# Another order of the steps on all engines: values of two head groups and the router product next to each other

## The reference

```python
def _L0_xattn_ref(query, key, value, Wq, bq, Wk, bk, Wv, bv, We, be, Wo, bo):
    Q = (query @ Wq.T + bq)...; K = (key @ Wk.T + bk)...; V = (value @ Wv.T + bv)...
    scores = jnp.einsum('bhqd,bhkd->bhqk', Q, K) / jnp.sqrt(jnp.asarray(DK, Q.dtype))
    attn = jax.nn.softmax(scores, axis=-1)
    out = jnp.einsum('bhqk,bhkd->bhqd', attn, V)
    expert = (jnp.einsum('bsd,eod->ebso', out, We) + be[:, None, None, :]).mean(axis=0)
    return expert @ Wo.T + bo

def _L0_ffn_ref(x, w_gate, w_expert, b_expert):
    probs = jax.nn.softmax(hs @ w_gate, axis=1)
    best = jnp.argmax(probs, axis=1)
    locations = jnp.cumsum(mask, axis=0) - 1      # only the first 100 rows of an expert count
    ...
    expert_out = dispatched @ w_expert + b_expert
    combined = combine.reshape(-1, E * C) @ expert_out

x = x + jnp.tanh(g_xattn[0]) * _L0_xattn_ref(_layernorm(x), ctx_1024, ctx_1024, ...)
x = x + jnp.tanh(g_ffn[0]) * _L0_ffn_ref(_layernorm(x), ...)
```

## Time and profile before

| | |
|---|---|
| median of 3 runs | 405.21 us (405.14 to 405.38) |
| the profiled execution: its own time | 405.64 us |
| its span, first to last instruction | 403.9 us, 8706 instructions |
| PE busy | 396.3 us (98%) |
| DVE busy | 333.3 us (83%) |
| ACT busy | 225.3 us (56%) |
| POOL busy | 167.4 us (41%) |
| granted TensorE clock | full in all 40 slices |

### The profile page before, as it was taken

The page is one execution under the profiler, slowest core; times in us unless marked ns, Lnnn a source line. Parts: engine busy times, 40 slices in busy tenths (PEclk is TensorE's granted clock), DMA queues, the critical chain, the costliest instruction groups (busy, mean ns, idle before and its releaser), DMA issues.

```text
span 403.9 us, 8706 instructions
## 1 busy us (share of the span) xinstructions
PE 396.3 (98%) x3102; PEld 182.2 (45%) x3102; DVE 333.3 (83%) x662; ACT 225.3 (56%) x320; POOL 167.4 (41%) x157
## 2 busy tenths in 40 slices
PE   7999999999999999999999999999999999899996
PEld 4556454443444444444444434444444444354444
DVE  6548456986898989998998998899897589779996
ACT  4436323568566754947485486748556474775110
POOL 2028999215080247309033530713271064460371
PEclk9999999999999999999999999999999999999999
DMA  8999991466059408823960692295169016241585
GB/s 278 334 389 394 344 390 41 91 124 165 2 111 199 174 1 170 217 98 85 175 223 1 142 238 104 60 183 189 54 133 242 5 33 175 84 132 28 99 172 180
DMA packets 65901, 63.19 MB, mean 156 GB/s; under 512 B 42277, under 2 KB 45617, under 8 KB 65859
## 3 DMA queue, kind: packets, MB, share of 16 engines
q1 hardware_dynamic: 60747, 56.19, 50.9%
q0 software_dynamic: 1632, 3.49, 3.1%
q10 hardware_dynamic: 3480, 2.96, 2.2%
HBM read 29.59 MB, written 12.98 MB: 105 GB/s over the span
## 4 chain that ended last, share of the span: by engine, by line
PE 71%; DVE 2%; issue 1%; ACT 1%; POOL 1%; DVEq 0%; ACTq 0%; POOLq 0%
PE ps L840 71%; ACT probs L1234 1%; PE ps L1161 0%; DVE xb L1567 0%; POOL known L1929 0%; POOL rstd L1929 0%; DVE bn_raw L1573 0%; ACT xn_hi L1234 0%; DVE xn L1500 0%; DVE base_cnt L1653 0%; DVE place_hot L1723 0%; POOL veps L1927 0%; ACT part_x L1234 0%; DVE xb L1865 0%; DVE wqT_lo L1678 0%
## 5 line engine op out<-in xcount | busy, mean ns | idle before, releaser
L1234 ACT ACTIVATE probs<-ps 120x1024 f32<-120x1024 f32 x64 | 62.0, 1024 | 19.4 <-PE ps L840 19.4
L1602 DVE TENSOR_REDUCE neg_max<-ps 128x16 bf16<-128x1920 f32 x32 | 68.7, 2148 | 3.7 <-PE ps L840 3.7
L1989 POOL TENSOR_TENSOR attn_lo<-attn,attn_hi 128x512 f16<-128x512 f32 x28 | 31.8, 1158 | 91.0 <-ACT attn_hi L1234 91.0
L840 PE MATMUL ps<-xnT_hi,wqT_hi 128*128 128x512 f16 x128 | 48.6, 380 | 0.0
L840 PE MATMUL ps<-mixT_hi,attn_hi 128*128 128x512 f16 x128 | 48.5, 379 | 0.0
L840 PE MATMUL ps<-mixT_lo,attn_hi 128*128 128x512 f16 x128 | 48.5, 379 | 0.0
L840 PE MATMUL ps<-xnT_lo,wqT_hi 128*128 128x512 f16 x128 | 48.5, 379 | 0.0
L1997 POOL TENSOR_TENSOR xb<-xb,mix_bias 128x512 f32<-128x512 f32 x32 | 39.6, 1271 | 15.4 <-DVE cb_col L1544 15.4
L1234 ACT ACTIVATE q_hi<-ps,bias_cols 128x512 f16<-128x512 f32 x32 | 22.1, 692 | 31.4 <-PE ps L840 31.4
L840 PE MATMUL ps<-q_stack,k_stack 97*128 97x512 f16 x128 | 33.9, 381 | 1.2 <-ACT probs L1234 1.0
L840 PE MATMUL ps<-probs,den_sel 120*32 120x256 f32 x512 | 34.1, 384 | 0.0
(11 more groups left out here) (279 smaller groups left out, 792.7 us busy)
## 6 DMA issues: line engine op xcount, KB each, us to landing
xb<-in_x_dram SPq DMA_DIRECT2D x8, 1024.0 KB, 6.1
q_stack<-q_hi SPq DMA_DIRECT2D x48, 128.0 KB, 2.4
out_dram<-xb SPq DMA_DIRECT2D x6, 1024.0 KB, 7.4
raw<-in_L_xattn_We_dram SPq DMA_DIRECT2D x5, 1024.0 KB, 10.3
q_stack<-q_lo SPq DMA_DIRECT2D x32, 128.0 KB, 2.4
xb<-in_L_xattn_We_dram SPq DMA_DIRECT2D x3, 1024.0 KB, 10.3
k_stack<-k_scratch SPq DMA_DIRECT2D x8, 360.0 KB, 4.6
k_scratch<-k_hi ACTq DMA_DIRECT2D x16, 120.0 KB, 7.9
```

The lines of the kernel that those rows point to most:

```text
L840: return e.matmul(out_, a, b, start=start, stop=stop, **kw)
L1234: return e.activation(out_, in_, func, **kw)
L1602: e.tensor_reduce(maxed[:, :, :, g], quad[:, :, 0:NT * SK].rearrange("p j (t s) -> p t j s", t=NT), AX.X, ALU.max, negate=True).then_inc(s ...
L1989: e.tensor_tensor(attn_lo[:, g, :], attn[:, g, :], attn_hi[:, g, :], ALU.subtract).then_inc(s_alo, 1)
```

## The change

The same steps stand in another order in the lists of TensorE, ScalarE, VectorE and GpSimd; SP's list stays. On TensorE, steady batches do `values` 0, `values` 1 and `route_x` between `scores` 1 and `scores` 2, with no scores between the two values, and split `q_tile` 0 around `places` and `scores` 3. Second last batch: `values` 0, `route_x`, `values` 1; both last `values` next to each other; spreads, mix steps, `logits` and `places` earlier against the scores and the shift. First: `route_x` after `max_scores` 1. ScalarE copies the router product before the next exp and does `x_hi` later; VectorE chooses the expert before the first norm's statistics and spreads `normalise1`, `x_lo`, `enter_rows` and `enter_places` over the batch; GpSimd adds the bias one batch earlier, ahead of both powers. One wait is added: the first late unit waits for the copy of the router product, with which it shares a bank. In the diff below "..." stands for the old lists of ScalarE and VectorE, which the functions above show, and blank lines and twelve leading blanks are dropped.

```diff
--- before.py
+++ after.py
@@ -843,6 +843,8 @@
     u = units[i]
     for s_, n in u["free"]:
         e.wait_ge(s_, n)
+    if i == N_FIRST:
+        e.wait_ge(s_pxe, 1)
     if u["done"] == made[("k", 0, 0)]:
         warm(u["bank"], NT)
         warm(u["bank"], NT)
@@ -1122,37 +1124,30 @@
     return prepare, 1, N_FIRST + i
 run([-1], [
-    (q_tile, 1, 0), (q_begin, 1, 1), (max_scores, 1, 0), (q_end, 1, 1), (route_x, 1, 0), (q_tile, 1, 2),
-    (max_scores, 1, 1),
-    (q_tile, 1, 3), (max_scores, 1, 2), late_unit(0), (max_scores, 1, 3), late_unit(1), (max_turn, 1, 0),
-    late_unit(2), late_unit(3), (scores, 1, 0), late_unit(4), late_unit(5),
+    (q_tile, 1, 0), (q_begin, 1, 1), (max_scores, 1, 0), (q_end, 1, 1), (q_tile, 1, 2),
+    (max_scores, 1, 1), (route_x, 1, 0), (q_tile, 1, 3), (max_scores, 1, 2), late_unit(0),
+    (max_scores, 1, 3), late_unit(1), (max_turn, 1, 0), late_unit(2), late_unit(3), (scores, 1, 0),
+    late_unit(4), late_unit(5),
 ])
 run(range(0, B - 2), [
-    (logits, -1, 0), (table_rows, -2, 0), (scores, 0, 1), (values, 0, 0), (scores, 0, 2),
-    (values, 0, 1), (route_x, 1, 0), (scores, 0, 3), (q_begin, 1, 0), (gate_mix, 0, 0),
-    (q_end, 1, 0), (places, -1, 0), (values, 0, 2), (values, 0, 3), (max_scores, 1, 0),
-    (q_tile, 1, 1), (q_begin, 1, 2), (spread_rden, 0, 0), (spread_rden, 0, 1), (q_end, 1, 2),
-    (max_scores, 1, 1), (spread_rden, 0, 2), (spread_rden, 0, 3), (q_tile, 1, 3),
-    (mix_high, 0, 0), (max_scores, 1, 2), (mix_low, 0, 0), (mix_high, 0, 1),
-    (max_scores, 1, 3), (route_attn, 0, 0), (mix_low, 0, 1), (mix_begin, 0, 2), (max_turn, 1, 0),
-    (mix_middle, 0, 2), (mix_low, 0, 2), (mix_high, 0, 3), (scores, 1, 0), (mix_low, 0, 3),
+    (logits, -1, 0), (table_rows, -2, 0), (scores, 0, 1), (values, 0, 0), (values, 0, 1),
+    (route_x, 1, 0), (scores, 0, 2), (q_begin, 1, 0), (gate_mix, 0, 0), (places, -1, 0),
+    (scores, 0, 3), (q_end, 1, 0), (values, 0, 2), (values, 0, 3), (max_scores, 1, 0), (q_tile, 1, 1),
+    (q_begin, 1, 2), (spread_rden, 0, 0), (spread_rden, 0, 1), (q_end, 1, 2), (max_scores, 1, 1),
+    (spread_rden, 0, 2), (spread_rden, 0, 3), (q_tile, 1, 3), (mix_high, 0, 0), (max_scores, 1, 2),
+    (mix_low, 0, 0), (mix_high, 0, 1), (max_scores, 1, 3), (route_attn, 0, 0), (mix_low, 0, 1),
+    (mix_begin, 0, 2), (max_turn, 1, 0), (mix_middle, 0, 2), (mix_low, 0, 2), (mix_high, 0, 3),
+    (scores, 1, 0), (mix_low, 0, 3),
 ])
 run([B - 2], [
-    (logits, -1, 0), (table_rows, -2, 0), (scores, 0, 1), (values, 0, 0), (scores, 0, 2),
-    (values, 0, 1), (route_x, 1, 0), (scores, 0, 3), (q_begin, 1, 0),
-    (places, -1, 0), (q_end, 1, 0), (values, 0, 2), (max_scores, 1, 0), (values, 0, 3),
-    (q_tile, 1, 1), (q_begin, 1, 2), (spread_rden, 0, 0), (spread_rden, 0, 1), (q_end, 1, 2),
-    (max_scores, 1, 1), (spread_rden, 0, 2), (spread_rden, 0, 3), (q_tile, 1, 3),
-    (mix_high, 0, 0), (max_scores, 1, 2), (mix_low, 0, 0), (mix_high, 0, 1),
-    (max_scores, 1, 3), (route_attn, 0, 0), (mix_low, 0, 1), (mix_begin, 0, 2), (max_turn, 1, 0),
-    (mix_middle, 0, 2), (logits, 0, 0), (mix_low, 0, 2), (mix_high, 0, 3), (scores, 1, 0),
-    (mix_low, 0, 3), (table_rows, -1, 0), (places, 0, 0),
+    (logits, -1, 0), (table_rows, -2, 0), (scores, 0, 1), (values, 0, 0), (route_x, 1, 0),
+    (values, 0, 1), (places, -1, 0), (scores, 0, 2), (q_begin, 1, 0), (q_end, 1, 0), (scores, 0, 3),
+    (values, 0, 2), (values, 0, 3), (max_scores, 1, 0), (q_tile, 1, 1), (spread_rden, 0, 0),
+    (spread_rden, 0, 1), (q_begin, 1, 2), (max_scores, 1, 1), (q_end, 1, 2), (spread_rden, 0, 2),
+    (q_tile, 1, 3), (spread_rden, 0, 3), (max_scores, 1, 2), (mix_high, 0, 0), (mix_low, 0, 0),
+    (max_scores, 1, 3), (route_attn, 0, 0), (mix_high, 0, 1), (mix_begin, 0, 2), (mix_low, 0, 1),
+    (logits, 0, 0), (mix_middle, 0, 2), (max_turn, 1, 0), (mix_low, 0, 2), (mix_high, 0, 3),
+    (places, 0, 0), (scores, 1, 0), (mix_low, 0, 3), (table_rows, -1, 0),
 ])
 def row_turn(_, x_):
     e.wait_ge(s_txn, x_ + 1)
@@ -1389,32 +1384,24 @@
 late_unit = lambda i: (prepare, 1, N_FIRST + i)
 run([-1], [
...
+    (q_high, 1, 0), (q_high, 1, 1), (q_high, 1, 2), (sum_high, 1, 0), (route_x_out, 1, 0),
+    (q_high, 1, 3), (stack_q, 1, 0), (x_hi, 2, 0), late_unit(1), (x_hi, 2, 1), (shift_row, 1, 0),
+    (stack_q, 1, 1), late_unit(2), late_unit(3), (x_hi, 2, 2), (x_hi, 2, 3), (exp, 1, 0), late_unit(4),
+    late_unit(5),
 ])
 run(range(0, B - 2), [
...
+    (exp, 0, 1), (value_out, 0, 0), (route_x_out, 1, 0), (exp, 0, 2), (value_out, 0, 1), (exp, 0, 3),
+    (q_high, 1, 0), (gate_mix_high, 0, 0), (gate_exp, -1, 0), (value_out, 0, 2), (value_out, 0, 3),
+    (x_hi, 2, 0), (rden_high, 0, 0), (x_hi, 2, 1), (q_high, 1, 1), (q_high, 1, 2), (attn_high, 0, 0),
+    (attn_high, 0, 1), (x_hi, 2, 2), (attn_high, 0, 2), (attn_high, 0, 3), (q_high, 1, 3),
+    (stack_q, 1, 0), (stack_q, 1, 1), (shift_row, 1, 0), (x_hi, 2, 3), (part_high, 0, 0), (exp, 1, 0),
 ])
 run([B - 2], [
...
+    (exp, 0, 1), (value_out, 0, 0), (route_x_out, 1, 0), (exp, 0, 2), (value_out, 0, 1), (exp, 0, 3),
+    (value_out, 0, 2), (gate_exp, -1, 0), (q_high, 1, 0), (rden_high, 0, 0), (value_out, 0, 3),
+    (q_high, 1, 1), (attn_high, 0, 0), (attn_high, 0, 1), (q_high, 1, 2), (attn_high, 0, 2),
+    (q_high, 1, 3), (attn_high, 0, 3), (stack_q, 1, 0), (expert_high, 1, 0), (stack_q, 1, 1),
+    (shift_row, 1, 0), (exp, 1, 0),
 ])
 run([B - 1], [
     (exp, 0, 1), (value_out, 0, 0), (gate_exp, -1, 0), (exp, 0, 2), (value_out, 0, 1),
@@ -1745,43 +1732,34 @@
 late_unit = lambda i: (prepare, 1, N_FIRST + i)
 run([-1], [
...
+    (q_low, 1, 0), (maxima, 1, 0), (q_low, 1, 1), (maxima, 1, 1), (q_low, 1, 2), (sum_low, 1, 0),
+    (sum_low, 1, 1), (maxima, 1, 2), (q_low, 1, 3), (normalise1, 2, 0), (maxima, 1, 3),
+    (normalise1, 2, 1), (sum_low, 1, 2), (x_lo, 2, 0), late_unit(0), (x_lo, 2, 1), late_unit(1),
+    (normalise1, 2, 2), (normalise1, 2, 3), (sum_low, 1, 3), (x_lo, 2, 2), (scale_bias, 1, 0),
+    late_unit(2), (x_lo, 2, 3), late_unit(3), late_unit(4), late_unit(5),
 ])
 run(range(0, B - 2), [
...
+    (logit_sum, -1, 0), (stats2, -1, 2), (stats2, -1, 3), (logit_gap, -1, 0), (choose, -1, 0),
+    (stats1, 2, 0), (add_table, -2, 0), (stats1, 2, 1), (moments2, -1, 0), (stats1, 2, 2),
+    (stats1, 2, 3), (moments1, 2, 0), (normalise1, 2, 0), (normalise1, 2, 1), (normalise1, 2, 2),
+    (logit_scale, -1, 0), (read_places, -1, 0), (gate_mix_low, 0, 0), (gate_value, -1, 0),
+    (q_low, 1, 0), (normalise1, 2, 3), (reciprocal, 0, 0), (maxima, 1, 0), (x_lo, 2, 0),
+    (rden_low, 0, 0), (q_low, 1, 1), (x_lo, 2, 1), (divide, 0, 0), (divide, 0, 1), (enter_rows, -1, 0),
+    (divide, 0, 2), (q_low, 1, 2), (divide, 0, 3), (maxima, 1, 1), (q_low, 1, 3), (maxima, 1, 2),
+    (x1_tile, 0, 0), (maxima, 1, 3), (stats2, 0, 0), (x1_tile, 0, 1), (route_sum, 0, 0), (x_lo, 2, 2),
+    (enter_places, -1, 0), (x_lo, 2, 3), (part_low, 0, 0), (stats2, 0, 1), (x1_tile, 0, 2),
     (x1_tile, 0, 3),
 ])
 run([B - 2], [
...
+    (logit_sum, -1, 0), (add_table, -2, 0), (stats2, -1, 2), (logit_gap, -1, 0), (stats2, -1, 3),
+    (choose, -1, 0), (moments2, -1, 0), (logit_scale, -1, 0), (read_places, -1, 0), (reciprocal, 0, 0),
+    (gate_value, -1, 0), (q_low, 1, 0), (rden_low, 0, 0), (maxima, 1, 0), (divide, 0, 0),
+    (q_low, 1, 1), (divide, 0, 1), (maxima, 1, 1), (divide, 0, 2), (q_low, 1, 2), (divide, 0, 3),
+    (maxima, 1, 2), (q_low, 1, 3), (x1_tile, 0, 0), (enter_rows, -1, 0), (route_sum, 0, 0),
+    (maxima, 1, 3), (enter_places, -1, 0), (logit_sum, 0, 0), (x1_tile, 0, 1), (logit_gap, 0, 0),
+    (choose, 0, 0), (stats2, 0, 0), (stats2, 0, 1), (x1_tile, 0, 2), (read_places, 0, 0),
+    (stats2, 0, 2), (x1_tile, 0, 3), (add_table, -1, 0), (stats2, 0, 3), (enter_token, 0, 0),
+    (enter_places, 0, 0), (moments2, 0, 0), (expert_low, 1, 0),
 ])
 def row_index(b, _):
@@ -1998,17 +1976,24 @@
     ins.then_inc(s_xbias, 1)
 def clear_rows(b, _):
+    if b != 1:
+        return
     prologue_over(e)
     e.wait_ge(s_mg, 1)
     e.memset(rows[:, :, :], 0.0).then_inc(s_clr, 1)
     e.memset(row_ix[:, :], 0).then_inc(s_clr, 1)
-attn_lows = [(attn_low, 0, g) for g in range(NK)]
-batch = [(rstd1, 2, 0), (rstd2, -1, 0)] + attn_lows + [(add_bias, 1, 0)]
-run(range(-1, 2), batch)
-clear_rows(0, 0)
-run(range(2, B - 2), batch)
-run([B - 2], [(rstd2, -1, 0)] + attn_lows + [(add_bias, 1, 0)])
+run([-1], [
+    (rstd1, 2, 0), (add_bias, 1, 0),
+])
+run(range(0, B - 2), [
+    (add_bias, 1, 0), (rstd2, -1, 0), (rstd1, 2, 0), (attn_low, 0, 0), (attn_low, 0, 1),
+    (attn_low, 0, 2), (attn_low, 0, 3), (clear_rows, 0, 0),
+])
+run([B - 2], [
+    (add_bias, 1, 0), (rstd2, -1, 0), (attn_low, 0, 0), (attn_low, 0, 1), (attn_low, 0, 2),
+    (attn_low, 0, 3),
+])
 e.wait_ge(s_clr, 2)
 e.indirect_dma_start(
     out=rows[:, 0, :], out_offset=None, in_=x_flat[:, :],
```

42 lines of the change are left out of this document (removed).

## The result

The changed kernel takes 406.48 us in the median of 7 runs (406.16 to 407.63), the kernel before 405.17 beside it (404.77 to 405.40): ratio 1.0038, 95% interval 1.0026 to 1.005. Forecast was 403.2.

The account below looks back on a forecast made before the run. TensorE was taken as the bound, busy 35.99 of 36 us in a steady batch. Front end 0.58, steady batches 0.6 and tail 0.8 summed to 2.0 off 405.21, giving 403.2 us, range 401.9 to 405.9.

Parts of the forecast that it names:

- Prologue: Before the steady batches: one change of shape fewer saves 0.11, a mix unit no longer waiting saves 0.43.
- Low transpose, 0.45: End of prologue: first low transpose issued later, landing 5.3 after its issue, so TensorE loses 0.25 to 0.65, taken as 0.45.
- the stay: TensorE's time on narrow-shape products; entering costs 0.09, leaving 0.11, so one fewer per steady batch saves 0.20.
- Steady batch, 0.12: Batches r = 0 to 5: 0.20 saved, less 0.01, 0.01 and 0.05 of waits, rounded to 0.12 each.
- the ties: Steady-batch waits taken back: 0.01 for ScalarE's bank copy, 0.01 before scores 3, 0.05 for VectorE before third maxima products.
- B: ScalarE late in steady batches: values 1 or scores 3 wait 0.25 in each of six, 404.7 us; chance 0.14.
- D: Changes of TensorE's shape are worth only half what was priced, giving 404.0 us; chance 0.08.
- E: Values 1 waits in full for its bank, 0.6 in each of six batches, giving 406.8 us; chance 0.02.
- "Nobody waits": GpSimd adds the bias one batch earlier in its idle time, four adds of 1.3 us, costing 0.
- rival A: VectorE becomes the bound around the third normalisation, reciprocal and maxima; 0.6 late in five batches gives 406.2 us; chance 0.16.
- Tail, 0.8: Last batch: moving half the expert's low part behind the moments, and row entries earlier, ends third scores 0.8 sooner.
- rival C: The tail gains nothing because the shift row's DMA sets the next scores, giving 404.0 us; chance 0.16.

Follow-up runs that it names:

- e10: Changed kernel with ScalarE's last two splits of x in the prologue put ahead of mix unit 3: 405.25 us, ratio 1.0.
- e1: Changed kernel with VectorE's `scale_bias`, which starts GpSimd's adds, moved behind the last `x_lo` in the prologue: 406.34 us, ratio 1.0018.
- e16: Changed kernel with scores 2 between values 1 and `route_x` in steady batches, ScalarE's third exp ahead of the router copy: 409.26 us, ratio 1.0089.
- e12: Kernel before with only TensorE's values 0, values 1, `route_x` put together in steady batches, `places` left behind `q_end`, ScalarE adapted: 412.35 us, ratio 1.0157.
- e2: Changed kernel with GpSimd's `clear_rows` put behind the next `add_bias`, as in the kernel before: 405.36 us, ratio 0.9997.
- e3: Changed kernel with VectorE's first `expert_low` moved behind `enter_values` in the last batch: 405.72 us, ratio 1.0004.
- e14: Changed kernel with two cures: ScalarE's splits of x sooner, `expert_low` behind `enter_values`: 404.50 us, ratio 0.9970.
- e15: Changed kernel with two cures: `clear_rows` behind the next `add_bias`, `expert_low` behind `enter_values`: 404.25 us, ratio 0.9966.
- e11: Changed kernel with all three cures: splits of x sooner, `clear_rows` behind the next `add_bias`, `expert_low` behind `enter_values`: 410.63 us, ratio 1.0121.
- e17: The changed kernel with all three cures (splits, `clear_rows`, `expert_low`) run once more: 410.83 us, ratio 1.0142.
- e13: Changed kernel with two cures: ScalarE's splits of x sooner, `clear_rows` behind the next `add_bias`: 404.13 us, ratio 0.9958.
- e8: Changed kernel with extra GpSimd work, adds in r = 3 and 5, memsets in r = 4, to price VectorE steps beside each: 414.97 us (one run).

## Why the prediction was wrong, point by point

- **Prologue** (forecast 0.11 + 0.43 sooner): too large. The mix unit's wait went in every trace, but first Q product to S(0) fell from 28.15 (28.14 to 28.27 in five traces of the old prologue) to 28.00. Worth 0.15: the change of shape gave 0.09, the wait 0.28 (18.43 - 17.94 from the turn of the maxima to the unit, counted from Q, became 18.27 - 18.06), and about 0.2 went back, most of it because the turn itself now starts 2.75 behind the unit ahead of it instead of 2.60. S(0) was 0.56 earlier in the first trace, which looked like my number; 0.41 of it was the start of the loads.
- **Low transpose, 0.45**: the step that failed in r = 0, worth 1.06 (36.76 against e10's 35.70). I let it take 5.3 from its own issue, from one row, and expected one loss; the mix copy's wait (0.49) I had not seen at all. e1 takes VectorE's part away and leaves r = 0 as long, e10 moves ScalarE's splits, which came 1.7 later than before, and the loss is gone: they held both transposes. Cured, r = 0 takes 35.70, 0.48 less than before: that is the 0.31 and 0.20 of the gate product and the stay.
- **Steady batch, 0.12**: right in kind, 0.07 in size. The stay is worth 0.21 (e16), about 0.10 for each change of shape as in the rows, and not the 0.05 of the rule set beside them; by difference the ties took 0.14 and not 0.07, of it 0.11 before the third maxima products, where I had 0.05. The idle of 1.48 on VectorE before the normalisation came, and did no harm. Rivals B, D and E did not happen in the changed kernel; a late ScalarE, as in B, is what e12 shows.
- **"Nobody waits" for GpSimd's `add_bias`: 0.** The step that failed and cost the sign. I asked who waits for a result, not who shares a way to memory. The new VectorE order has `x_lo` and `place_hot` at 158.8 to 161.3 and `clear_rows` pushes the next adds into them: 1.27 by e2. The result on the clock is what rival A described (VectorE the bound, slower), in one batch instead of five, and for another reason.
- **Tail, 0.8**: 0.48, and 1.18 with `expert_low` moved (e3). I had priced `expert_low` behind the moments as free; it held GpSimd's first step for 0.87. Behind T the trace of e3 is 0.2 longer than the others (52.5), those of e14 and e15 are not. The forecast mechanism was right, rival C was not: scores of the last batch waited 0.26 for the shift row, not 0.8 to 1.6, and behind them TensorE waits for the exponentials all the same (0.31). The 3.74 that I read for this DMA runs up to scores before which no wait stands; from issue to landing it took 3.38 in that trace and 2.21 in the changed kernel's.
- **Sum**: forecast -2.0. The cut gives -0.15 + 0.58 + 1.21 + 0.04 - 0.48 for the single stages and -0.15 for r = 2 to 5 together: +1.05. With two cures -0.9 to -1.6 was measured; with all three the distance from Q to T is 1.5 (e11) and 1.7 (e17) shorter than before, and by my estimate would be 1.8 to 2.2 with the r = 1 of e13 (36.09). That is near the 2.0 I had forecast, but in part by luck: the prologue and the steady batches gave less than I had, the tail more. No kernel here has all of it at its end.

## What to carry to other kernels

When steps are moved on VectorE or GpSimd, lay the two engines' timelines over each other and mark each VectorE step by where its inputs lie. In these runs a step with two SBUF inputs was held by GpSimd's adds and not by its memset, `TENSOR_SCALAR` from SBUF to SBUF was held by both, and steps that read PSUM kept their lengths, as did the statistics of a tile in SBUF (0.68 at 156.93, beside the adds of r = 1). Price a meeting by the rest of the other engine's instruction (1.3 an add, 3.5 the memset here), not by the step's own length. And compare traces by the distance between marks behind the loads; the start of S(0) agreed with my forecast here by luck.

## What was not expected of the hardware

- The pairs of e8: 0.18 became 1.26 beside adds and 0.17 beside a memset; 1.46 became 4.74 beside a memset. It works both ways: GpSimd's 0.23 became 1.10 beside a two-input VectorE step of 1.19. The same section of the Trainium skill (SBUF — State Buffer, Who interferes with whom) says that `tensor_scalar` can enter a two-port mode, in which VectorE contends with GpSimd for the port pair they share, and that whoever issues first gets it for the whole instruction; the 4.74 agrees.
- Two DMA transposes of one size, issued 2.0 to 2.8 apart: the second landed 4.3 to 6.1 after its issue at the end of the prologue, and no fixed time from either issue, nor the gap between them, told when.
- The halt of e11 and e17, 7.1 us with the half clock behind it, from three changes of which any two are harmless: the cause is open.
